# Edge scores of a graph layer: rings of six groups for four, and GpSimd's gathers written out

## The chip, the cores and the metric

The kernel runs on one core of one Trainium2 chip. Its engines are TensorE (PE), VectorE (DVE), ScalarE (ACT), GpSimd (POOL) and SyncE (SP, which here only issues DMAs). The metric is the device time of one execution in microseconds (us). The median of three runs is 2775.32 us (2767.02 to 2775.95).

## The reference, cut to what matters

The kernel computes two layers over a graph of 3125 nodes and 53125 edges, the edges sorted by their target node:

```python
x = x + _L0_gnn_ref(_layernorm(x), edge_index, edge_attr_64, ...)
x = x + _L0_ffn_ref(_layernorm(x)[None], ...)[0]
x = x + _L1_gnn_ref(_layernorm(x), ..., src, dst)
x = x + _L1_ffn_ref(_layernorm(x)[None], ...)[0]
```

Only the first of these, the attention over edges, has the stage that changes:

```python
Q = (x @ Wq).reshape(N, 8, 32); K = (x @ Wk).reshape(N, 8, 32)
score = (Q[src] * K[tgt]).sum(axis=-1) * scale + edge_attr @ We
```

A softmax over the edges of each target, a weighted sum of V rows and the other three parts follow. The change leaves them as they are.

## The kernel before, in words

The stage before has written the query rows to DRAM (`q_rows`, 3125 rows of 1 KB) and the key rows, split into three bf16 parts and packed by rank, to `k_rows`. It has put the source nodes of all edges into SBUF as `src_t`: 128 partitions by 86 groups by 5 indices. Then comes the edge stage, lines 658 to 944. 128 edges stand one per partition, and five such columns make one group of 640 edges; there are 84 groups (`NK`). Every engine but SP runs a loop of 21 turns of four groups (`EITER`, `GI`), and SP three pieces of such a loop. The buffers that carry a group are rings of four: `qr` (query rows), `ea` and `eaT` (edge attributes and their transposes), `loc` (places of key rows) and the one-hot tiles `oh_lo` and `oh_hi`.

One group n goes like this:

- ACT waits until DVE has freed group n-2 (wait at L812), copies the 5 indices of group n+2 from `src_t` to the ring `src_s` (L788, "staging") and signals GpSimd. Then it copies the transposed edge attributes out of PSUM (L816, L817), makes its half of the key one-hots of group n+1 (L797, L801), and copies the score of the edge attributes (L823).
- GpSimd waits for the staged indices and issues five indirect DMAs (L766), each of which gathers 128 query rows of 1 KB into `qr`. Since ACT stages in program order, a gather of group n+2 starts only after ACT has finished group n-1. The gathers of groups 0 and 1 (L368) belong to the stage before.
- PE loads five start positions into registers (L845), transposes the edge attributes (L852), selects key rows with 20 one-hot matmuls into three PSUM banks of `psK` (L864), multiplies the edge attributes by We (L873) and counts source nodes (L879).
- DVE makes its half of the key one-hots (L899) and the counting one-hots (L927, L929), waits for the gathered rows and for each bank of `psK`, multiplies `qr` by it in place (L934, three per group) and adds up each head (L939). That last instruction raises `s_free`, which frees the group's slot.
- SP loads the edge attributes of group n (L724, L725, L727) when PE has transposed group n-4, and `loc` of group n+1 (L735).

At the start of the stage SP and ACT also load the key rows into SBUF (`kp`, L711).

The order of the work is fixed by the order of the code on each engine and by semaphores; no planner chooses it.

Of the kernel before, what the change touches and what calls it, by code (L numbers as in the profile page):

```python
# [6 lines left out]
BF16 = mybir.dt.bfloat16  # L7
# [22 lines left out]
AHEAD = 2  # L30
R = 42
# [38 lines left out]
def build(nc, x, src, dst, edge_attr_64, L0_gnn_Wq, L0_gnn_Wk, L0_gnn_Wv, L0_gnn_We, L0_gnn_Wo, L0_gnn_bo,  # L70
# [7 lines left out]
    def sb_high(ctx, name, shape, dt=F32):  # L78
        return ctx.enter_context(nc.sbuf_tensor(name, shape, dt, side="right"))
# [4 lines left out]
    def sem(name):  # L84
        return top.enter_context(nc.semaphore(name))
# [7 lines left out]
    with top:  # L93
# [567 lines left out]
        s_webd, s_ea = sem1("we_loaded"), [sem1(f"ea{g}_loaded") for g in range(GI)]  # L661
        s_staged, s_open = sem1("indices_staged"), sem1("gathers_open")
        s_loc = [sem1(f"locals{g}_loaded") for g in range(GI)]
# [7 lines left out]
        with ExitStack() as st:  # L671
            we2 = sb(st, "we2", [2 * ED, 2 * H])
            src_s = sb(st, "src_s", [E, GI, G], I32)
            kp = sb(st, "kp", [3 * R, KB, D], BF16)
            loc = sb(st, "loc", [3 * R, GI, G * E], BF16)
# [5 lines left out]
            ea = sb(st, "ea", [E, GI, G * ED])  # L681
            eaT = sb(st, "eaT", [128, GI, 3 * E])
# [4 lines left out]
            oh_lo = sb(st, "oh_lo", [E, GI, G, P], BF16)  # L687
            oh_hi = sb(st, "oh_hi", [E, GI, G, T], BF16)
# [12 lines left out]
            K_SLOT = (0, 1, 0, 1)  # L701
# [13 lines left out]
            def _(sp):  # L715
# [4 lines left out]
                def load_ea(i, g, tail):  # L720

                    at = bass.ds((i * GI * G + g * G) * ED, G * ED)
                    sp.wait_ge(s_ead, i * GI + g + 1)
# [22 lines left out]
                with sp.Fori(last_i + 1, EITER) as i:  # L746
# [12 lines left out]
            @block.gpsimd  # L759
            def _(pool):  # L760
                def gather(n, g):

                    pool.wait_ge(s_staged, n + g - AHEAD + 1)
                    pool.sem_inc(s_open, 1)
                    for u in range(G):
                        nc.gpsimd.indirect_dma_start(  # L766
                            out=qr[:, g, u, :], out_offset=None, in_=q_rows,
                            in_offset=bass.IndirectOffsetOnAxis(ap=src_s[:, g, u:u + 1], axis=0)).then_inc(s_got[g], 16)

                for g in range(AHEAD, GI):  # L770
                    gather(0, g)
                with pool.Fori(1, EITER) as i:
                    for g in range(GI):
                        gather(i * GI, g)

                for s in sems0:
                    pool.sem_clear(s)

            @block.scalar
            def _(act):  # L780
# [3 lines left out]
                act.sem_inc(s_eae, GI)  # L784
                act.sem_inc(s_esk, GI)

                def stage(at, g):
                    nc.scalar.activation(src_s[:, g, :], src_t[:, at, :].rearrange("p a u -> p (a u)"), ACT.Copy)\  # L788
                      .then_inc(s_staged, 1)

                def k_onehots(slot, k_slot, turn):

                    act.wait_ge(s_loc[slot], 16 * (turn + 1))
                    act.wait_ge(s_kta, turn * GI + slot + GI)
# [4 lines left out]
                    act.wait_ge(s_kabs, turn * GI + slot + 1)  # L799
# [4 lines left out]
                act.sem_inc(s_kta, GI)  # L804
# [4 lines left out]
                with act.Fori(0, EITER) as i:  # L809
                    for g in range(GI):  # L810
# [12 lines left out]
                        nc.scalar.activation(score[:, :, bass.ds(i * GI * G + g * G, G)].rearrange("p h u -> p u h"),  # L823
# [12 lines left out]
            def _(pe):  # L836
# [4 lines left out]
                pe.sem_inc(s_ead, GI)  # L841
                pe.sem_inc(s_ohu, GI)
                with pe.Fori(0, EITER) as i:
                    for g in range(GI):
                        _, first = nc.values_load_multi_w_load_instructions(  # L845
                            base_i[0:1, bass.ds(i * GI * G + g * G, G)], engines=[mybir.EngineType.PE], min_val=0, max_val=KB - CB)

                        pe.wait_ge(s_ea[g], 48 * (i + 1))
                        pe.wait_ge(s_eae, i * GI + previous_use(g, 2, GI) + 1 + GI)
# [6 lines left out]
                        pe.wait_ge(s_kt, i * GI + g + 1 + GI)  # L856
                        pe.wait_ge(s_kta, i * GI + g + 1 + GI)
                        if g in K_GROUPS:
                            pe.wait_ge(s_kp[K_GROUPS.index(g)], 48)
                        for m, (a, b) in enumerate(BANKS):  # L860
                            pe.wait_ge(s_kfree, (i * GI + g) * 3 + m + 1)
# [7 lines left out]
                        pe.wait_ge(s_eae, i * GI + g + 1 + GI)  # L869
                        pe.wait_ge(s_esk, i * GI + previous_use(g, 2, GI) + 1 + GI)  # L870
# [6 lines left out]
                        pe.wait_ge(s_oh, i * GI + g + 1)  # L877
# [7 lines left out]
                pe.wait_ge(s_free, GI + NK)  # L885
# [8 lines left out]
            def _(v):  # L894
# [7 lines left out]
                v.sem_inc(s_free, GI)  # L902
# [15 lines left out]
                v.sem_inc(s_kt, GI)  # L918
                v.sem_inc(s_kfree, 3)
                k_onehots(0, K_SLOT[0], 0)  # L920
                with v.Fori(0, EITER) as i:
                    for g in range(GI):
# [9 lines left out]
                        for m, (a, b) in enumerate(BANKS):  # L932
                            v.wait_ge(s_kx, (i * GI + g) * 3 + m + 1)
# [3 lines left out]
                        v.wait_ge(s_kfree, (i * GI + g) * 3 + 6)  # L937
# [1217 lines left out]
```

## Time and profile before

| | |
|---|---|
| median of three runs | 2775.32 us |
| profiled execution, its span | 2767.3 us |
| fastest of the three runs | 2767.02 us |
| edge stage, from first gather L766 to last | 165.6 to 857.4 us |
| mean granted clock of TensorE over the span | 0.724 of full |

The profile shows one execution. Its own time is its span of 2767.3 us, which is within 0.3 us of the fastest run, so nothing of note lies around the span. A timeline row gives the start of an instruction, its length, its engine, its line and tiles, and in brackets how long the engine had been idle before it and what ended that. "remote" means that a semaphore ended the wait and the profile does not name a sender that had just finished. "issue" means that it waited for nothing that the profile shows. The time of a gather is the time in which GpSimd writes its descriptors; its data move later.

### The profile page before, as it was taken

How to read it: one execution, taken by the hardware profiler on the slowest of the kernel's cores; microseconds unless marked ns; L12 is line 12 of the kernel's file. 1: busy time of each engine (PE TensorE's matmuls, PEld its weight loads, DVE VectorE, ACT ScalarE, POOL GpSimd, SP SyncE). 2: the span in 40 equal slices, each digit the busy share in tenths (PEclk: the TensorE clock that was granted, in tenths of full speed). 3: DMA queues.
4: the chain of work that ended last, by engine and by line, in shares of the span. 5: the costliest groups of instructions: out<-in, count | busy, mean ns of one | idle time of the engine just before them, and what ended most of it. 6: DMA issues, size and time to landing. Idle time of an engine off the chain costs nothing. (4 is left out here: it accounts for less than half of the span.)

```text
span 2767.3 us, 37014 instructions
## 1 busy us (share of the span) xinstructions
PE 1553.5 (56%) x9103; PEld 1290.4 (47%) x9104; DVE 1112.4 (40%) x2670; ACT 770.1 (28%) x1831; POOL 1089.8 (39%) x1126
## 2 busy tenths in 40 slices
PE   6347777777786478699940000000004747999992
PEld 5235555555564356489940000000003647999992
DVE  6335555555554743211133333333334773112123
ACT  4234444444443134233411000000000123334440
POOL 0635555555662020022215666666665001222220
PEclk9757666666656689799975555555556958999996
DMA  4384443444443310066644455555553017999997
GB/s 122 97 156 114 116 117 114 113 120 111 119 118 89 82 35 28 6 194 193 207 130 153 165 187 193 180 167 176 168 197 109 0 47 257 335 341 347 336 344 196
DMA packets 264204, 434.41 MB, mean 157 GB/s; under 512 B 36520, under 2 KB 203960, under 8 KB 264039
## 3 DMA queue, kind: packets, MB, share of 16 engines
q1 hardware_dynamic: 203011, 289.15, 32.6%
q0 software_dynamic: 54768, 141.45, 17.5%
q10 hardware_dynamic: 6388, 3.39, 0.7%
q8 instruction: 15, 0.25, 0.0%
q14 instruction: 22, 0.18, 0.0%
HBM read 342.48 MB, written 91.37 MB: 157 GB/s over the span
## 5 line engine op out<-in xcount | busy, mean ns | idle before, releaser
L766 POOL DMA_INDIRECT qr<-q_rows,src_s x410 | 404.1, 986 | 328.8 <-ACT src_s L788 219.5
L1796 POOL DMA_INDIRECT fr<-f_rows,src_s x420 | 407.0, 969 | 259.1 <-ACT src_s L1787 129.7
L2079 PE MATMUL psO<-acc,carry_on 128*125 128x256 f32 x50 | 21.9, 620 | 692.9 <-DVEq L1975 677.4
L864 PE MATMUL psK<-kp,oh_k 126*128 x1680 | 351.9, 373 | 68.6 <-issue 67.8
L1816 DVE SCALAR_TENSOR_TENSOR acc<-acc,same,fr 128x256 f32<-128x256 f32 x420 | 203.6, 485 | 413.4 <-issue 262.1
L2079 PEld LDWEIGHTS psO<-acc,carry_on 128*125 128x125 f32 x50 | 15.4, 321 | 699.0 <-DVEq L1975 677.8
L864 PEld LDWEIGHTS psK<-kp,oh_k 126*128 126x128 bf16 x1680 | 217.1, 129 | 194.6 <-issue 114.8
L934 DVE TENSOR_TENSOR qr<-qr,psK 128x512 f32<-128x512 f32 (+1 forms) x252 | 141.0, 594 | 299.4 <-remote 190.5
L1617 PEld LDWEIGHTS m1psH<-m1xT,m1w 128*128 128x128 f32 x1792 | 211.4, 194 | 2.8
L1617 PE MATMUL m1psH<-m1xT,m1w 128*128 128x128 f32 x1792 | 211.6, 277 | 0.0
L1629 PE MATMUL m1psY<-m1w,m1hT 128*128 128x256 f32 x896 | 203.4, 380 | 1.0 <-issue 0.6
L1597 ACT ACTIVATE m1hT<-m1psH,m1par 128x128 f32<-128x128 f32 x448 | 128.1, 369 | 249.4 <-PE m1psH L1617 169.4
L1787 ACT ACTIVATE src_s<-src_i 128x5 int32 x84 | 17.5, 208 | 583.8 <-DVEq L1823 293.5
L1629 PEld LDWEIGHTS m1psY<-m1w,m1hT 128*128 128x128 f32 x896 | 165.8, 190 | 23.1 <-issue 2.2
L1571 POOL DMA_INDIRECT y<-m1yr,m1to x56 | 54.8, 979 | 289.6 <-DVE m1yr L1680 289.6
L797 ACT ACTIVATE dist<-loc,k_neg 126x640 bf16<-126x640 bf16 x170 | 130.9, 821 | 31.7 <-DMA loc<-locals_ 31.7
L852 PE MATMUL psE<-ident,ea 128*128 128x128 f32 (+1 forms) x252 | 63.2, 378 | 130.1 <-issue 110.5
L939 DVE TENSOR_REDUCE dots<-qr 128x1280 f32 x84 | 125.0, 1488 | 18.6 <-DVE qr L934 14.4
L1617 PEld LDWEIGHTS m0psH<-m0xT,m0w 128*128 128x128 f32 x1024 | 120.9, 194 | 1.5
L1617 PE MATMUL m0psH<-m0xT,m0w 128*128 128x128 f32 x1024 | 121.0, 277 | 0.0
L801 ACT ACTIVATE oh_k<-dist,ones 126x1280 bf16<-126x1280 bf16 x85 | 115.8, 1363 | 10.1
L1629 PE MATMUL m0psY<-m0w,m0hT 128*128 128x256 f32 x512 | 115.8, 379 | 0.0
(447 smaller groups left out, 2456.4 us busy)
## 6 DMA issues: line engine op xcount, KB each, us to landing
m1w<-in_L_ffn_W_dram SPq DMA_DIRECT2D x112, 1024.0 KB
run_rows<-acc SPq DMA_DIRECT2D x84, 640.0 KB
m0w<-in_L_ffn_Wd_dram SPq DMA_DIRECT2D x32, 1024.0 KB, 5.5
loc<-locals_ SPq DMA_DIRECT2D x85, 157.5 KB
ea<-in_edge_attr_dram SPq DMA_DIRECT2D x84, 140.0 KB
yt<-y SPq DMA_DIRECT2D x15, 560.0 KB
m1b<-in_L_ffn_b_dram SPq DMA_DIRECT2D x56, 128.0 KB
fr<-f_rows,src_s POOLq DMA_INDIRECT x420
```

Of the source, the lines that this page charges most:

```text
L766: nc.gpsimd.indirect_dma_start(out=qr[:, g, u, :], out_offset=None, in_=q_rows, in_offset=bass.IndirectOffsetOnAxis(ap=src_s[:, g, u:u + 1 ...
L797: last = nc.scalar.activation(dist[:, c - CD, :], loc[:, slot, :], ACT.Abs, bias=k_neg[:, c:c + 1])
L801: nc.scalar.activation(oh_k[:, k_slot, CD:CB, :], dist[:], ACT.Relu, bias=ones[0:3 * R, 0:1], scale=-1.0)\
L852: last = nc.tensor.transpose(psE[0:w, g % 2, n * E:(n + 1) * E], ea[:, g, n * 128:n * 128 + w], ident[:])
L864: last = nc.tensor.matmul(psK[:, m, (u - a) * D:(u - a + 1) * D], oh_k[:, K_SLOT[g], c, u * E:(u + 1) * E], kp[:, bass.ds(first[u] + c, 1) ...
L934: nc.vector.tensor_tensor(qr[:, g, a:b].rearrange("p u d -> p (u d)"), qr[:, g, a:b].rearrange("p u d -> p (u d)"), psK[:, m, 0:(b - a) * ...
L939: nc.vector.tensor_reduce(dots[:, :, at].rearrange("p h u -> p u h"), qr[:, g].rearrange("p u (h d) -> p u h d", h=H), AX.X, ALU.add).then ...
L1597: last = nc.scalar.activation(hT[s][:, m, :], psH[s][:, m * 128:(m + 1) * 128], ACT.Gelu, bias=par[s][:, m:m + 1] if own_w1 else b1_0[:, m ...
L1617: last = nc.tensor.matmul(psH[s][:, m * 128:(m + 1) * 128], w1[s if own_w1 else 0][:, k, m * 128:(m + 1) * 128], xT[s][:, k, :], start=(k ...
L1629: last = nc.tensor.matmul(psY[:, s, 0:D], hT[s][:, m, :], w2[s][:, m, :], start=(m == 0), stop=(m == KC - 1))
L1796: nc.gpsimd.indirect_dma_start(out=fr[:, g, u, :], out_offset=None, in_=f_rows, in_offset=bass.IndirectOffsetOnAxis(ap=src_s[:, g, u:u + 1 ...
L1816: ins = nc.vector.scalar_tensor_tensor(acc[:, g, u, :], acc[:, n // G % GI, n % G, :], same[:, bass.ds(i * GI * G + g * G + u, 1)], fr[:, ...
```

## The change

Six groups take the place of four in the rings and loops of the edge stage (`GB`, `BITER` for `GI`, `EITER`): 14 turns of six. `src_s` and ACT's staging go. GpSimd's loop goes too: its 82 groups of five gathers stand in the program one after another, take their indices from `src_t` directly, and wait for `s_free`, that is, for DVE having freed group n-6. The later gather stage (L1796) keeps its rings of four.

```diff
 AHEAD = 2
+GB = 6
+BITER = NK // GB
...
-        s_got = [sem(f"rows{g}_gathered") for g in range(GI)]
+        s_got = [sem(f"rows{g}_gathered") for g in range(GB)]
         qr_ctx = ExitStack()
-        qr = sb_high(qr_ctx, "qr", [E, GI, G, D])
+        qr = sb_high(qr_ctx, "qr", [E, GB, G, D])
...
-        s_staged, s_open = sem1("indices_staged"), sem1("gathers_open")
-        s_loc = [sem1(f"locals{g}_loaded") for g in range(GI)]
+        s_webd, s_ea = sem1("we_loaded"), [sem1(f"ea{g}_loaded") for g in range(GB)]
+        s_loc = [sem1(f"locals{g}_loaded") for g in range(GB)]
...
-            src_s = sb(st, "src_s", [E, GI, G], I32)
-            loc = sb(st, "loc", [3 * R, GI, G * E], BF16)
+            loc = sb(st, "loc", [3 * R, GB, G * E], BF16)
...
-            ea = sb(st, "ea", [E, GI, G * ED])
-            eaT = sb(st, "eaT", [128, GI, 3 * E])
+            ea = sb(st, "ea", [E, GB, G * ED])
+            eaT = sb(st, "eaT", [128, GB, 3 * E])
...
-            oh_lo = sb(st, "oh_lo", [E, GI, G, P], BF16)
-            oh_hi = sb(st, "oh_hi", [E, GI, G, T], BF16)
+            oh_lo = sb(st, "oh_lo", [E, GB, G, P], BF16)
+            oh_hi = sb(st, "oh_hi", [E, GB, G, T], BF16)
...
-            K_SLOT = (0, 1, 0, 1)
+            K_SLOT = (0, 1) * (GB // 2)
...
-                    sp.wait_ge(s_kt, i * GI + g + 2)
-                    sp.wait_ge(s_kta, i * GI + g + 2)
-                    sp.dma_start(loc[:, (g + 1) % GI, :], locals_[bass.ds((i * GI + g + 1) * G * E, G * E)]
-                                 .partition_broadcast(3 * R)).then_inc(s_loc[(g + 1) % GI], 16)
-
-                last_i, last_g = REST // G // GI, REST // G % GI
+                    sp.wait_ge(s_kt, i * GB + g + 2)
+                    sp.wait_ge(s_kta, i * GB + g + 2)
+                    sp.dma_start(loc[:, (g + 1) % GB, :], locals_[bass.ds((i * GB + g + 1) * G * E, G * E)]
+                                 .partition_broadcast(3 * R)).then_inc(s_loc[(g + 1) % GB], 16)
...
             def _(pool):
-                def gather(n, g):
-
-                    pool.wait_ge(s_staged, n + g - AHEAD + 1)
-                    pool.sem_inc(s_open, 1)
+                for n in range(AHEAD, NK):
+                    pool.wait_ge(s_free, n + 1)
                     for u in range(G):
-                        nc.gpsimd.indirect_dma_start(
-                            out=qr[:, g, u, :], out_offset=None, in_=q_rows,
-                            in_offset=bass.IndirectOffsetOnAxis(ap=src_s[:, g, u:u + 1], axis=0)).then_inc(s_got[g], 16)
-
-                for g in range(AHEAD, GI):
-                    gather(0, g)
-                with pool.Fori(1, EITER) as i:
-                    for g in range(GI):
-                        gather(i * GI, g)
+                        nc.gpsimd.indirect_dma_start(out=qr[:, n % GB, u, :], out_offset=None, in_=q_rows,
+                                                     in_offset=bass.IndirectOffsetOnAxis(ap=src_t[:, n, u:u + 1], axis=0))\
+                          .then_inc(s_got[n % GB], 16)
 
                 for s in sems0:
                     pool.sem_clear(s)
...
-                def stage(at, g):
-                    nc.scalar.activation(src_s[:, g, :], src_t[:, at, :].rearrange("p a u -> p (a u)"), ACT.Copy)\
-                      .then_inc(s_staged, 1)
...
-                with act.Fori(0, EITER) as i:
-                    for g in range(GI):
-
-                        act.wait_ge(s_free, i * GI + g + AHEAD + 1)
-                        act.sem_inc(carrier, 1)
-                        stage(bass.ds(i * GI + g + AHEAD, 1), (g + AHEAD) % GI)
-                        act.wait_ge(s_ead, i * GI + g + 1 + GI)
+                with act.Fori(0, BITER) as i:
+                    for g in range(GB):
+                        act.wait_ge(s_ead, i * GB + g + 1 + GB)
                         nc.scalar.activation(eaT[:, g, 0:2 * E], psE[:, g % 2, 0:2 * E], ACT.Copy)
                         nc.scalar.activation(eaT[0:ED, g, 2 * E:3 * E], psE[0:ED, g % 2, 2 * E:3 * E], ACT.Copy)\
                           .then_inc(s_eae, 1)
 
-                        k_onehots((g + 1) % GI, K_SLOT[(g + 1) % GI], i + (g + 1) // GI)
-                        act.wait_ge(s_es, i * GI + g + 1)
+                        k_onehots((g + 1) % GB, K_SLOT[(g + 1) % GB], i + (g + 1) // GB)
+                        act.wait_ge(s_es, i * GB + g + 1)
...
-                        pe.wait_ge(s_eae, i * GI + g + 1 + GI)
-                        pe.wait_ge(s_esk, i * GI + previous_use(g, 2, GI) + 1 + GI)
+                        pe.wait_ge(s_eae, i * GB + g + 1 + GB)
+                        pe.wait_ge(s_esk, i * GB + previous_use(g, 2, GB) + 1 + GB)
...
-                v.sem_inc(s_free, GI)
+                v.sem_inc(s_free, GB)
...
-                with v.Fori(0, EITER) as i:
-                    for g in range(GI):
-                        at = bass.ds(i * GI * G + g * G, G)
-
-                        k_onehots((g + 1) % GI, K_SLOT[(g + 1) % GI], i + (g + 1) // GI)
-                        v.wait_ge(s_ohu, i * GI + g + 1)
+                with v.Fori(0, BITER) as i:
+                    for g in range(GB):
+                        at = bass.ds(i * GB * G + g * G, G)
```

Wherever the diff is cut, `GI` becomes `GB` and `EITER` becomes `BITER` in the same way.

On GpSimd, the edge stage before is this. `indices_staged` is ACT's signal, and L777 clears semaphores:

```order
L759 UNCONDITIONAL_BRANCH [waits barrier_Pool_Activation_PE_DVE_SP_gather]
L766 DMA qr<-q_rows,src_s 128x256 [waits indices_staged]
L766 DMA qr<-q_rows,src_s 128x256 x4
...
L772 UNCONDITIONAL_BRANCH
L772 ISA
L766 DMA qr<-q_rows,src_s 128x256 [waits indices_staged]
L766 DMA qr<-q_rows,src_s 128x256 x4
...
L763 REGISTER_ALU
L766 DMA qr<-q_rows,src_s 128x256 [waits indices_staged]
L766 DMA qr<-q_rows,src_s 128x256 x4
...
L772 REGISTER_ALU
L772 COMPARE_AND_BRANCH
L777 ISA x50
```

After the change the stage is 82 times the same five gathers without a branch; the wait is DVE's `rows_free`:

```order
L759 UNCONDITIONAL_BRANCH [waits barrier_Pool_Activation_PE_DVE_SP_gather]
L764 DMA qr<-q_rows,src_t 128x256 [waits rows_free]
L764 DMA qr<-q_rows,src_t 128x256 x4
...
L764 DMA qr<-q_rows,src_t 128x256 [waits rows_free]
L764 DMA qr<-q_rows,src_t 128x256 x4
L769 ISA x50
L672 UNCONDITIONAL_BRANCH
```

So GpSimd no longer waits for ACT, and its instructions stand once for each group where before four groups stood in a loop.

On ACT, the first group of the loop before, from the start of the loop to the score:

```order
L809 UNCONDITIONAL_BRANCH
...
L788 ISA [waits rows_free]
L788 ACTIVATE src_s<-src_t 128x5
...
L816 ACTIVATE eaT<-psE 128x256 [waits ea_turned]
L817 ACTIVATE eaT<-psE 64x128
...
L797 ACTIVATE dist<-loc,k_neg 126x640 [waits locals1_loaded,k_onehots_act]
...
L801 ACTIVATE oh_k<-dist,ones 126x1280 [waits k_distances]
...
L823 ISA [waits edge_score_done]
L823 ACTIVATE score<-psS 128x5x8
```

and after:

```order
L797 UNCONDITIONAL_BRANCH
...
L800 ACTIVATE eaT<-psE 128x256 [waits ea_turned]
L801 ACTIVATE eaT<-psE 64x128
...
L785 ACTIVATE dist<-loc,k_neg 126x640 [waits locals1_loaded,k_onehots_act]
...
L789 ACTIVATE oh_k<-dist,ones 126x1280 [waits k_distances]
...
L807 ISA [waits edge_score_done]
L807 ACTIVATE score<-psS 128x5x8
```

The wait for `rows_free` and the staging copy are gone from ACT; everything behind them moves up.

## Rows read from the trace of the kernel before

**Rows 1.** The page: engines (busy, share, instructions), and the group of gathers

```profile
PE 1553.5 (56%) x9103; PEld 1290.4 (47%) x9104; DVE 1112.4 (40%) x2670; ACT 770.1 (28%) x1831; POOL 1089.8 (39%) x1126
...
L766 POOL DMA_INDIRECT qr<-q_rows,src_s x410 | 404.1, 986 | 328.8 <-ACT src_s L788 219.5
```

**Rows 2.** Waits, 160 to 875 us: who waited for whom, total us, times, longest

```profile
POOL qr L766 <- ACT src_s L788: 219.5, 56, 40.1
DVE qr L934 <- remote: 190.5, 39, 9.4
...
POOL qr L766 <- issue: 109.3, 354, 1.2
```

**Rows 3.** Tile qr: count, min/median/max ns, first and last start

```profile
L766 POOL DMA_INDIRECT qr<-q_rows,src_s x410: 943/949/1602, 165.6 to 857.4; - x137
...
L939 DVE TENSOR_REDUCE dots<-qr x84: 1487/1489/1491, 167.4 to 871.3; 128x1280 f32 x84
```

**Rows 4.** Timeline of POOL, 530 to 562 and 566 to 576 us

```profile
531.12 0.95 POOL L766 DMA_INDIRECT qr<-q_rows,src_s  x1 [2.10 <-ACT src_s L788]
...
542.40 0.95 POOL L766 DMA_INDIRECT qr<-q_rows,src_s  x1 [0.30 <-issue]
549.08 0.95 POOL L766 DMA_INDIRECT qr<-q_rows,src_s  x1 [5.72 <-ACT src_s L788]
...
557.67 0.94 POOL L766 DMA_INDIRECT qr<-q_rows,src_s  x1 [2.64 <-ACT src_s L788]
...
569.40 0.95 POOL L766 DMA_INDIRECT qr<-q_rows,src_s  x1 [0.30 <-issue]
```

**Rows 5.** Timeline of DVE, the same stretches

```profile
545.51 1.62 DVE L934 TENSOR_TENSOR qr<-qr,psK 128x512 f32<-128x512 f32 x3 [7.78 <-remote]
547.35 1.49 DVE L939 TENSOR_REDUCE dots<-qr 128x1280 f32 x1 [0.22 <-DVE qr L934]
...
556.88 1.49 DVE L939 TENSOR_REDUCE dots<-qr 128x1280 f32 x1 [0.22 <-DVE qr L934]
...
561.72 1.49 DVE L939 TENSOR_REDUCE dots<-qr 128x1280 f32 x1 [0.22 <-issue]
...
571.95 1.62 DVE L934 TENSOR_TENSOR qr<-qr,psK 128x512 f32<-128x512 f32 x3 [7.23 <-remote]
```

**Rows 6.** Timeline of ACT, 534 to 562 us

```profile
544.65 0.38 ACT L816 ACTIVATE eaT<-psE 128x256 f32<-128x256 f32 x1 [8.41 <-remote]
...
548.10 0.20 ACT L788 ACTIVATE src_s<-src_t 128x5 int32 x1
```

**Rows 7.** Timeline of PE, 525 to 562 us

```profile
528.91 0.87 PE L852 MATMUL psE<-ident,ea 128*128 128x128 f32 x3 [1.92 <-issue]
...
535.72 0.88 PE L852 MATMUL psE<-ident,ea 128*128 128x128 f32 x3
```

**Rows 8.** Start of the stage: timeline of all engines, 120 to 182 us

```profile
161.84 0.90 PE L852 MATMUL psE<-ident,ea 128*128 128x128 f32 x3 [15.71 <-DMA ea<-in_edge_attr_dram]
```

**Rows 9.** Window: PE, PEld, DVE, ACT, POOL busy, granted clock, DMA share, GB/s

```profile
146.00:162.00 16.00, 0.28 (x2) 0.19 (x3) 0.00 (x0) 0.00 (x0) 0.00 (x0) 0.50 1.08 168
```

**Rows 10.** DMA queues, 160 to 872 us: packets, MB, share of 16 engines

```profile
q0 software_dynamic: 19680, 53.77, 26.9%
...
q14 instruction: 2, 0.02, 0.0%
```

**Rows 11.** Gathers written out, next stage: timeline of all engines, 955 to 994 us

```profile
983.76 1.23 PE L185 MATMUL psT<-ident,tile_a 125*128 125x125 f32 x10
...
988.89 1.34 ACT L193 ACTIVATE tT<-psT 128x500 f32<-128x500 f32 x3 [11.01 <-remote]
```

**Rows 12.** First written-out gathers, L368: timeline of all engines, 66 to 100 us

```profile
69.75 1.12 POOL L368 DMA_INDIRECT qr<-q_rows,src_t  x1 [62.02 <-DMA q_rows<-x]
...
80.73 0.95 POOL L368 DMA_INDIRECT qr<-q_rows,src_t  x1 [0.30 <-issue]
80.82 0.19 DVE L588 TENSOR_TENSOR pre<-pre,has_in 125x25 f32<-125x25 f32 x1
```

More of the change, by code:

```diff
@@ L783, in _ @@
                 act.dma_start(we2[ED:2 * ED, H:2 * H], L0_gnn_We).then_inc(s_webd, 16)
-                act.sem_inc(s_eae, GI)
-                act.sem_inc(s_esk, GI)
-                def stage(at, g):
-                    nc.scalar.activation(src_s[:, g, :], src_t[:, at, :].rearrange("p a u -> p (a u)"), ACT.Copy)\
-                      .then_inc(s_staged, 1)
+                act.sem_inc(s_eae, GB)
+                act.sem_inc(s_esk, GB)
                 def k_onehots(slot, k_slot, turn):
                     act.wait_ge(s_loc[slot], 16 * (turn + 1))
-                    act.wait_ge(s_kta, turn * GI + slot + GI)
+                    act.wait_ge(s_kta, turn * GB + slot + GB)
                     act.sem_inc(carrier, 1)
@@ L798, in k_onehots @@
                     last.then_inc(s_kabs, 1)
-                    act.wait_ge(s_kabs, turn * GI + slot + 1)
+                    act.wait_ge(s_kabs, turn * GB + slot + 1)
                     act.sem_inc(carrier, 1)
@@ L808, in _ @@
                     load_k(act, n)
-                with act.Fori(0, EITER) as i:
-                    for g in range(GI):
-                        act.wait_ge(s_free, i * GI + g + AHEAD + 1)
-                        act.sem_inc(carrier, 1)
-                        stage(bass.ds(i * GI + g + AHEAD, 1), (g + AHEAD) % GI)
-                        act.wait_ge(s_ead, i * GI + g + 1 + GI)
+                with act.Fori(0, BITER) as i:
+                    for g in range(GB):
+                        act.wait_ge(s_ead, i * GB + g + 1 + GB)
                         nc.scalar.activation(eaT[:, g, 0:2 * E], psE[:, g % 2, 0:2 * E], ACT.Copy)
@@ L818, in _ @@
                           .then_inc(s_eae, 1)
-                        k_onehots((g + 1) % GI, K_SLOT[(g + 1) % GI], i + (g + 1) // GI)
-                        act.wait_ge(s_es, i * GI + g + 1)
+                        k_onehots((g + 1) % GB, K_SLOT[(g + 1) % GB], i + (g + 1) // GB)
+                        act.wait_ge(s_es, i * GB + g + 1)
                         act.sem_inc(carrier, 1)
-                        nc.scalar.activation(score[:, :, bass.ds(i * GI * G + g * G, G)].rearrange("p h u -> p u h"),
+                        nc.scalar.activation(score[:, :, bass.ds(i * GB * G + g * G, G)].rearrange("p h u -> p u h"),
                                              psS[:, g % 2, 0:G * H].rearrange("p (u h) -> p u h", h=H), ACT.Copy)\
@@ L840, in _ @@
                 nc.tensor.matmul(psC[0:P, 0:T], zb[:], zb[:, 0:T], start=True, stop=False, skip_group_check=True)
[L841 to L844, printed above, removed]
+                pe.sem_inc(s_ead, GB)
+                pe.sem_inc(s_ohu, GB)
+                with pe.Fori(0, BITER) as i:
+                    for g in range(GB):
                         _, first = nc.values_load_multi_w_load_instructions(
-                            base_i[0:1, bass.ds(i * GI * G + g * G, G)], engines=[mybir.EngineType.PE], min_val=0, max_val=KB - CB)
+                            base_i[0:1, bass.ds(i * GB * G + g * G, G)], engines=[mybir.EngineType.PE], min_val=0, max_val=KB - CB)
                         pe.wait_ge(s_ea[g], 48 * (i + 1))
-                        pe.wait_ge(s_eae, i * GI + previous_use(g, 2, GI) + 1 + GI)
+                        pe.wait_ge(s_eae, i * GB + previous_use(g, 2, GB) + 1 + GB)
                         for n in range(3):
@@ L917, in _ @@
                 dve_order.link(v, nc.vector.tensor_scalar(k_neg[:], k_at[:], -1.0, None, ALU.mult))
-                v.sem_inc(s_kt, GI)
+                v.sem_inc(s_kt, GB)
                 v.sem_inc(s_kfree, 3)
                 k_onehots(0, K_SLOT[0], 0)
-                with v.Fori(0, EITER) as i:
-                    for g in range(GI):
-                        at = bass.ds(i * GI * G + g * G, G)
-                        k_onehots((g + 1) % GI, K_SLOT[(g + 1) % GI], i + (g + 1) // GI)
-                        v.wait_ge(s_ohu, i * GI + g + 1)
+                with v.Fori(0, BITER) as i:
+                    for g in range(GB):
+                        at = bass.ds(i * GB * G + g * G, G)
+                        k_onehots((g + 1) % GB, K_SLOT[(g + 1) % GB], i + (g + 1) // GB)
+                        v.wait_ge(s_ohu, i * GB + g + 1)
                         nc.vector.tensor_tensor(oh_lo[:, g], iota_row[:].unsqueeze(1).to_broadcast([E, G, P]),
```

26 lines of the change are left out of this document (13 added, 13 removed).

## Prediction

> **What bounds the kernel now.** I read the page's shares first: no engine is busy for more than 56% of the span, so waits set the time, and the average over the stages says little of this one [rows 1]. Then I took the stage by itself. Its last result is the reduce of DVE, which frees a slot: 84 of them, the first starting at 167.4 us and the last at 871.3 [rows 3], 703.9 / 83 = 8.48 us per group. The list of waits of that stretch is next. DVE's longest waits stand before the multiply and end "remote"; no row there names a gather. So gathered rows are in time, and it is PE's products that are late. GpSimd waits for ACT's staging 56 times, 219.5 us, of which the longest, 40.1, lies ahead of its first gather [rows 2].
>
> That makes GpSimd a chain which adds up: 410 gathers x 0.986 us = 404.1 busy [rows 1], 109.3 of short gaps between them (354, 0.31 each) and 219.5 - 40.1 = 179.4 of waits [rows 2], together 692.8 us; the first gather starts at 165.6 and the last ends at 857.4 + 0.95 = 858.4 [rows 3], which is 692.8 too. 82 groups in 56 bursts are 1.46 groups per burst, with a mean pause of 3.2 us. Yet nobody waits for its rows. Why does the pace follow it? The timelines answer. A burst of two groups runs from 531.12 to 542.40 + 0.95 = 543.35 [rows 4]. In it PE's transposes begin at 535.72 and take 0.88 [rows 7], but ACT copies them only at 544.65, after 8.41 us of waiting that ends "remote" [rows 6], and DVE's multiply starts at 545.51 after 7.78 [rows 5]. The same after the next double burst: it ends at 569.40 + 0.95 = 570.35 [rows 4], the multiply starts at 571.95 [rows 5]. So what PE signals in a long burst arrives 2.16 and 1.60 us after its end. Signals of the first 4 us or so of a burst pass: transposes start 6.81 us apart (528.91, 535.72) across one burst's start [rows 7]. Between bursts and in a single one two reduces start 4.84 us apart (556.88, 561.72) [rows 5]. I read this as: descriptor writing on GpSimd holds up PE and its signals, and pauses are when the stage moves.
>
> **The change part by part.** The sum is against the profiled execution. Its span is 2767.3 us, its time equals the fastest of the three runs, 8 below the median 2775.32.
>
> *The staging on ACT goes*: 84 copies x 0.20 = 17 us of ACT [rows 6]. ACT is 28% busy [rows 1] and waits for PE's signal right behind each, so I cost it at nothing; were that cover gone, it would give back at most those 17 us.
>
> *Loops and rings of six.* 14 turns for 21 save 7 ends of turns per engine. No row shows one by itself; a group with such an end is within the 0.3 to 2 us of any "issue" gap [rows 4, 7], so 0 to 14 us, and PE's signals, not its issue, are waited for: I take 0. Loads of edge attributes may run six groups ahead instead of four; no wait of DVE names them. 0.
>
> *The first gathers move.* Today gather 2 starts at 165.6, after ACT has the loads behind it. Now slots 2 to 5 are free from the start, so 4 x 5 = 20 gathers go out as soon as GpSimd enters the stage, beside the loads of key rows. From 146 to 162 the DMA engines are full, 1.08 [rows 9], and PE's first transposes wait 15.71 us for edge attributes until 161.84 [rows 8]. A gather costs all 16 engines 26.9% x 712 us / 410 = 0.467 us [rows 10, 1], 20 of them 9.3. If they all go ahead of that load the stage starts 9.3 later, if behind it 0. I take the middle, 4.7, and keep both ends. The first reduce then ends at 167.4 + 1.49 + 4.7 = 173.6. The Trainium skill, "DMA: Bandwidth & Descriptors", section "Issuing engines are not separate DMA queues", says that DMAs started by the scalar, sync or gpsimd engine run on the same 16 engines and interleave. By that rule the shift would be nearer 9.3, and the result 4.6 later; no row here shows the two kinds side by side.
>
> *GpSimd's gate.* This is the term that decides. Today the pause ends when ACT stages, that is, when ACT has got through group n-1. In the new order it ends when DVE has freed group n-6. Per gather nothing changes: 0.986 and a 0.31 gap. Behind the waiting gather only gathers are queued, so the wait harms nobody by itself. But GpSimd, which today gets one group or two per staging, will write whatever slots are free. It reaches the full ring early (20 gathers at the start) and from there each reduce lets one group go. A group is 5 x 1.295 = 6.5 us of writing. The first reduce after a pause starts a burst 0.8 us later (today the staging copy ends at 548.30 and the gather starts at 549.08 [rows 6, 4]). The second reduce comes 4.8 to 6.8 us behind it, at DVE's free pace or PE's: before the first group is written out. So the burst doubles. The third group's products are signalled later than 4 us into the burst, and by the rows above they arrive after its end. So I expect bursts of two groups, always: 82 - 4 = 78 groups in 39 bursts. A pause is then 1.9 (mean of 2.16 and 1.60) for the signal, 3.3 from the multiply to the end of the reduce (545.51 to 547.35 + 1.49 = 548.84 [rows 5]), and 0.8 to the first gather: 6.0 us, against a mean of 3.2 today, where staging precedes the reduce.
>
> The sum: 78 x 5 x 0.986 = 384.5 busy; 351 gaps x 0.309 = 108.4; 38 pauses x 6.0 = 228.0; together 720.9. From the first gated gather, 173.6 + 0.8 = 174.4, to 895.3. Then 1.9 + 3.3 to the reduce that this burst held up, 900.5, and five groups still ahead with no gathers beside them, at PE's 6.8: 934.5. Today the stage's last reduce ends at 872.8. That is 61.7 later: 2767.3 + 61.7 = 2829.0. What follows waits for that reduce, so I let it pass on in full.
>
> Bounds of this term. If every burst is a single group whose successor is late, two in three groups cost 6.5 + 3.0, 9.5 each: about 20 more, 2849. If the pause is what it is today, 3.2, the 38 pauses lose 106 and the gain of the lookahead shows: 2723.
>
> **Rivals.**
> *B, bursts of three groups.* Six slots may let DVE free two slots in the pause. 26 bursts have 25 pauses: 13 fewer x 6.0 = 78, 2751. For it: the third reduce comes at 4.8 after the second if its products were finished before the burst [rows 5]. Against: the double burst of 531 held its second group's products back for 7.78 us.
> *C, the stall goes.* Perhaps it comes from GpSimd's loop or from the semaphores of the staging, and not from writing descriptors. Then PE's 6.8 per group bounds: 78 x 6.8 + 34 = 564 from 173.6, 738, 135 earlier: 2632. For it: in the first written-out gathers, from 69.75 on, DVE still does small steps in order with one at 80.82 while gathers go out [rows 12]. Against: these steps wait for DVE itself, and in the written-out gathers of the next stage PE's transposes, 983.76 + 1.23, are copied by ACT only at 988.89, 3.9 us late, after 11.01 of waiting [rows 11].
> *D, the pace stays.* The lookahead isn't used, since no rows were waited for; PE's chain goes on at 8.48 and the later start (4.7) and faster end cancel: about 2767.
> *E, code loading, on the slower side.* PE's turn grows from four groups to six, from some 300 instructions to some 450. In this stage only two instruction packets were fetched on q14 [rows 10], so today's loop is resident. If six groups are not, each of 13 returns fetches two blocks. The rows have no duration for that; between a gather's gap of 0.31 and PE's issue gap of 1.92 [rows 2, 7] I take the middle, 1.1: 13 x 2 x 1.1 = 29: 2796 without other effects. It decides once a turn no longer stays resident. The Trainium skill, "Runtime: NRT & Kernel Launch", section "Instruction fetch mechanics", says that a taken branch whose target isn't in the current two-page window forces a fetch of the target page. By that rule a larger turn is the risk; the present trace shows a turn of 300 without such fetches.
>
> **How the numbers follow.** The double bursts have 0.50, B 0.18, C 0.14, D 0.13, E 0.05. The predicted time is that of the likeliest, 2829; its own range is 2800 (a pause of 5.3) to 2850. The range 2740 to 2865 holds it, E, D and B, and some 16 more for a start 4.6 later and single bursts; C and the lower bound of the pause are left out. About 0.3%, 8 us, is what a measurement of this kernel tells from no change. Faster: B and C, 0.32. Within: D, 0.13. Slower: the first and E, 0.55.
>
> **What would show it.** In the new trace GpSimd's waits name DVE's reduce, about 38 times with a mean near 6 us; its bursts are of ten gathers; the last gather ends near 895 and the last reduce near 934; DVE's waits before the multiply still end "remote", and PE's signals arrive 1.6 to 2.2 us after a burst. The first transposes come after 161.84 by up to 9.3. The forecast is wrong if bursts are longer than 20 us with DVE working on within them (B, C), if the pause is 3 us or less, or if PE's "issue" gaps grow at each sixth group with new instruction packets (E).

## The result and the profile after

The changed kernel takes 2805.8 us (median of four runs, 2804.6 to 2812.8), the kernel before, measured with it, 2771.2: 1.0144 times as long, 95% interval 1.0108 to 1.0179. It is slower by about 35 us. The profiled execution has a span of 2811.0 us against 2767.3.

First the waits of the stage, which ran from 137 to 910 us; the rows are those of 140 to 915 us (engine, line, what it waited for: total us, times, longest). They answer to [rows 2]:

```profile
POOL qr L764 <- DVE dots L923: 235.2, 50, 17.5
DVE qr L918 <- remote: 205.9, 46, 8.3
...
POOL qr L764 <- issue: 109.2, 358, 0.3
```

GpSimd now waits for DVE's reduce, 50 times, and DVE's wait for late signals has grown from 190.5 us in 39 waits to 205.9 in 46. The tile `qr` shows where the stage begins and ends (min, median, max ns; first and last start). These rows answer to [rows 3], and the page's row of the gathers to [rows 1]:

```profile
L764 POOL DMA_INDIRECT qr<-q_rows,src_t x410: 943/949/1374, 137.5 to 870.7; - x137
L923 DVE TENSOR_REDUCE dots<-qr x84: 1487/1489/1491, 178.1 to 908.2; 128x1280 f32 x84
```

```profile
L764 POOL DMA_INDIRECT qr<-q_rows,src_t x410 | 389.5, 950 | 352.5 <-DVE dots L923 235.2
```

The first reduce is 10.7 us later (178.1 for 167.4), the last one 36.9 later (908.2 for 871.3). In between the pace is 730.1 / 83 = 8.80 us per group for 8.48. The remaining 43.7 - 36.9 = 6.8 us of the profile's difference fall behind the stage, where the code is the same; from the last reduce's end to the span's end the two kernels and the six others profiled on chips of this kind take 1884 to 1901 us, so those 6.8 lie within the scatter of eight profiles.

Now the timeline of the changed kernel from 292 to 322 us, three groups in the pattern that returns through most of the stage (start, length, engine, work, idle time before and what ended it). It answers to [rows 4 to 7]. POOL and DVE:

```profile
292.90 1.49 DVE L923 TENSOR_REDUCE dots<-qr 128x1280 f32 x1 [0.22 <-DVE qr L918]
294.66 0.95 POOL L764 DMA_INDIRECT qr<-q_rows,src_t  x1 [5.55 <-DVE dots L923]
...
299.67 0.95 POOL L764 DMA_INDIRECT qr<-q_rows,src_t  x1 [0.30 <-issue]
301.80 0.42 DVE L918 TENSOR_TENSOR qr<-qr,psK 128x256 f32<-128x256 f32 x1 [1.47 <-remote]
302.45 1.49 DVE L923 TENSOR_REDUCE dots<-qr 128x1280 f32 x1 [0.22 <-DVE qr L918]
304.21 0.95 POOL L764 DMA_INDIRECT qr<-q_rows,src_t  x1 [3.59 <-DVE dots L923]
307.23 1.49 DVE L923 TENSOR_REDUCE dots<-qr 128x1280 f32 x1 [0.23 <-DVE qr L918]
...
315.50 0.94 POOL L764 DMA_INDIRECT qr<-q_rows,src_t  x1 [0.30 <-issue]
318.39 1.62 DVE L918 TENSOR_TENSOR qr<-qr,psK 128x512 f32<-128x512 f32 x3 [8.11 <-PE psK L848]
320.22 1.49 DVE L923 TENSOR_REDUCE dots<-qr 128x1280 f32 x1 [0.22 <-DVE qr L918]
321.98 0.95 POOL L764 DMA_INDIRECT qr<-q_rows,src_t  x1 [5.54 <-DVE dots L923]
```

and PE in the double burst:

```profile
308.30 1.86 PE L848 MATMUL psK<-kp,oh_k 126*128 x11
...
310.62 0.27 PE L848 MATMUL psK<-kp,oh_k 126*128 x1 [0.46 <-issue]
311.37 0.28 PE L848 MATMUL psK<-kp,oh_k 126*128 x1 [0.48 <-issue]
312.74 0.41 PE L848 MATMUL psK<-kp,oh_k 126*128 x2 [1.09 <-issue]
```

Read it downwards. The reduce that ends at 294.39 lets a burst of one group go, 294.66 to 300.62. The third multiply of the next group gets its signal 1.2 us after that burst, so the next reduce comes 9.55 us after the first, when GpSimd has been idle for 3.59. It opens a burst of two groups, since the reduce after that comes 4.78 us later, in time. In this burst PE gets through 11 of 20 key matmuls in 1.86 us, then needs 7.4 us for the other nine (310.62 to 318.04); DVE's multiply begins 318.39 - 316.44 = 1.95 us after the last gather has ended, though PE had started the products of the first bank ten us before. Here PE itself is late, and the signal with it; the run with the late first gathers, below, shows a signal that is late after PE was done. Then the reduce, and 0.27 us later the next burst. Three groups take 9.55 + 4.78 + 12.99 = 27.3 us; before, such a turn of three was 26.4 us, from the reduce at 547.35 to the one at 573.79.

### The profile page after: what moved, and what is told of

Same layout as the page of the kernel before. It is cut to its first block and busy times, and to the rows that moved or that the text cites. A ratio compares the mean times of both kernels' runs of the same rounds, so it can differ in the third digit from the quotient of the medians.

```text
span 2811.0 us, 36475 instructions
## 1 busy us (share of the span) xinstructions
PE 1571.4 (56%) x9103; PEld 1292.4 (46%) x9104; DVE 1116.1 (40%) x2670; ACT 756.1 (27%) x1747; POOL 1079.1 (38%) x1126
## 5 line engine op out<-in xcount | busy, mean ns | idle before, releaser
L764 POOL DMA_INDIRECT qr<-q_rows,src_t x410 | 389.5, 950 | 352.5 <-DVE dots L923 235.2
L848 PEld LDWEIGHTS psK<-kp,oh_k 126*128 126x128 bf16 x1680 | 209.8, 125 | 235.4 <-issue 157.7
L918 DVE TENSOR_TENSOR qr<-qr,psK 128x512 f32<-128x512 f32 (+1 forms) x252 | 142.3, 594 | 322.8 <-remote 205.9
L1601 PEld LDWEIGHTS m1psH<-m1xT,m1w 128*128 128x128 f32 x1792 | 211.3, 194 | 2.8
L1601 PE MATMUL m1psH<-m1xT,m1w 128*128 128x128 f32 x1792 | 211.5, 277 | 0.0
L1601 PEld LDWEIGHTS m0psH<-m0xT,m0w 128*128 128x128 f32 x1024 | 121.8, 196 | 1.6
L1601 PE MATMUL m0psH<-m0xT,m0w 128*128 128x128 f32 x1024 | 121.9, 279 | 0.0
```

The source lines that it names most:

```text
L764: nc.gpsimd.indirect_dma_start(out=qr[:, n % GB, u, :], out_offset=None, in_=q_rows, in_offset=bass.IndirectOffsetOnAxis(ap=src_t[:, n, u: ...
L848: last = nc.tensor.matmul(psK[:, m, (u - a) * D:(u - a + 1) * D], oh_k[:, K_SLOT[g], c, u * E:(u + 1) * E], kp[:, bass.ds(first[u] + c, 1) ...
L918: nc.vector.tensor_tensor(qr[:, g, a:b].rearrange("p u d -> p (u d)"), qr[:, g, a:b].rearrange("p u d -> p (u d)"), psK[:, m, 0:(b - a) * ...
L1601: last = nc.tensor.matmul(psH[s][:, m * 128:(m + 1) * 128], w1[s if own_w1 else 0][:, k, m * 128:(m + 1) * 128], xT[s][:, k, :], start=(k ...
```

## The experiments

Twelve runs were made; eight stand in the table, the others in the text. They fall into five groups, each on another chip and each beside the kernel before. It took 2769.1 and 2770.9 us on two of these chips and 2517.7, 2520.0 and 2523.3 on the other three. I call the first a "chip of 2770" and the others a "chip of 2520". None of the five was met twice, so whether the chip or a state that it was in makes the difference is not shown.

| kernel | before there | median us | ratio, 95% interval | us per group |
|---|---|---|---|---|
| rings of six, staging kept | 2769.1 | 2771.1 | 1.0005 (0.9987 to 1.0023) | 8.46 |
| rings of four, written out, reduce gate | 2769.1 | 2802.8 | 1.0132 (1.0105 to 1.0160) | 8.89 |
| changed kernel + score gate | 2769.1 | 2752.8 | 0.9941 (0.9916 to 0.9966) | 8.22 |
| changed kernel, first gathers late | 2769.1 | 2825.8 | 1.0212 (1.0187 to 1.0237) | 9.13 |
| rows of 256 bytes | 2770.9 | 2816.2 | 1.0160 (1.0135 to 1.0184) | 8.85 |
| score gate again | 2770.9 | 2752.9 | 0.9925 (0.9902 to 0.9949) | 8.23 |
| no gathers past the ring | 2517.7 | 2520.3 | 0.9999 (0.9972 to 1.0026) | 6.34 |
| changed kernel again | 2520.0 | 2530.6 | 1.0042 (1.0017 to 1.0068) | 6.37 |

**Rings of six alone.** ACT's staging and GpSimd's loop of the kernel before, in the rings and turns of the changed one:

```diff
-                for n in range(AHEAD, NK):
-                    pool.wait_ge(s_free, n + 1)
+                def gather(n, g):
+                    pool.wait_ge(s_staged, n + g - AHEAD + 1)
...
+                with pool.Fori(1, BITER) as i:
+                    for g in range(GB):
+                        gather(i * GB, g)
```

> Rings of six and 14 turns, but ACT's staging and GpSimd's loop as before. If the place of GpSimd's gate makes the change slow (my theory): bursts, pauses and pace as before, 8.4 to 8.5 us per group, within 8 us of the kernel before. If rings of six or the longer turns cost (rival): about 8.8 us per group and 25 to 35 us over before.

Measured: no difference from before, 8.46 us per group, 57 bursts with a mean pause of 3.23 us (before 56 and 3.29). GpSimd's wait for the staging is the same as in [rows 2]:

```profile
POOL qr L768 <- ACT src_s L790: 218.9, 56, 40.8
```

The depth of the rings and the longer turns cost nothing and bring nothing. The rival falls, and with it code loading in turns of six: in the window of [rows 10], 160 to 872 us, four instruction packets came on q14 here and seven in the changed kernel, for two before, where two blocks at each of 13 returns would be 26.

**Written out with rings of four.**

```diff
-                    pool.wait_ge(s_staged, n + g - AHEAD + 1)
+                for n in range(AHEAD, NK):
+                    pool.wait_ge(s_free, n + 1)
...
+                        nc.gpsimd.indirect_dma_start(out=qr[:, n % GI, u, :], ...
```

> Rings of four as before, GpSimd's gathers written out, indices in place, gate on DVE's reduce of group n-4. Theory (the gate is after the reduce, the depth does not matter): 8.8 us per group, the start later by about 5 us (10 early gathers for 20), 25 to 35 us over before. If depth six is what makes it slow: 8.4 to 8.5 us per group and no more than 5 over before.

Measured: 33.7 us over before, as forecast. 80 gated groups went in 53 bursts with a mean pause of 4.38 us; in the changed kernel 78 groups in 50 bursts, 4.44. So this half of the change makes the whole loss, with rings of four as with rings of six. It still has three parts: the code written out, the indices in place, and the gate. The next one parts them.

**The gate moved back.** One line on top of the changed kernel:

```diff
                     pool.wait_ge(s_free, n + 1)
+                    pool.wait_ge(s_esk, GB + n - AHEAD)
```

> The changed kernel with one more wait on GpSimd: group n also waits for ACT's score of group n-3, which is where ACT's staging stood. Theory: mean pause back from 4.4 to about 3.3 us, gathers still 0.95 us each, so 8.2 to 8.4 us per group and 5 to 25 us under before. Rival (written-out code or reading the indices in place is what costs): 8.8 us per group, as the changed kernel.

Measured: 16.3 us under before, and 18.0 under on another chip. Code written out and indices read in place stay, so neither is what costs: it is the gate. The start differs from the changed kernel's too, because only five gathers now go out early for 20, and the first reduce comes at 172.7 us for 178.1. That is 5 us; the pace, 8.22 us per group for 8.80, is 48. The waits of its stage, and three rows of its timeline where a burst begins:

```profile
POOL qr L765 <- ACT score L808: 180.6, 56, 26.4
DVE qr L919 <- remote: 157.8, 37, 9.3
```

```profile
424.83 0.24 ACT L808 ACTIVATE score<-psS 128x40 f32 x1 [1.19 <-PE psS L858]
425.75 1.49 DVE L924 TENSOR_REDUCE dots<-qr 128x1280 f32 x1 [0.22 <-DVE qr L919]
425.82 0.94 POOL L765 DMA_INDIRECT qr<-q_rows,src_t  x1 [2.44 <-ACT score L808]
```

The gather begins at 425.82, beside the reduce that starts at 425.75. With the reduce as the gate it would have begun after 427.24; with the 0.27 us seen above that is some 1.7 us later, an estimate. The mean pause is 2.90 us over 57 pauses of the gated part, less than before's 3.29. That no staging copy stands between ACT's signal and the gather any more fits this, but no run shows it by itself. This is the version that beats both kernels, on the chips of 2770; on those of 2520 it was not run.

**The first gathers later.**

```diff
+                pool.wait_ge(s_ead, GB + 1)
                 for n in range(AHEAD, NK):
```

> The changed kernel, but GpSimd's first gather of the stage waits for PE's first transposes. If the 20 early gathers delay the load of edge attributes: transposes back at 162 us for 172.5, and 5 to 11 us under the changed kernel (less than 10.7 where the 25 us burst then falls beside the first groups). If the later start has another reason: transposes still at 170 or later.

Measured: 1.0212 times before for the changed kernel's 1.0144, so some 19 us slower than it, outside both expectations in sign. The transposes did move, to 167.5 us, and the first reduce to 173.5 for 178.1. But now the first burst runs beside the work:

```profile
173.54 1.49 DVE L924 TENSOR_REDUCE dots<-qr 128x1280 f32 x1 [0.22 <-issue]
...
185.00 0.37 PE L849 MATMUL psK<-kp,oh_k 126*128 x1 [0.95 <-issue]
...
191.98 0.38 ACT L801 ACTIVATE eaT<-psE 128x256 f32<-128x256 f32 x1 [12.92 <-remote]
...
203.94 1.62 DVE L919 TENSOR_TENSOR qr<-qr,psK 128x512 f32<-128x512 f32 x3 [27.37 <-remote]
205.78 1.49 DVE L924 TENSOR_REDUCE dots<-qr 128x1280 f32 x1 [0.22 <-DVE qr L919]
```

```profile
168.64 1.04 POOL L765 DMA_INDIRECT qr<-q_rows,src_t  x1 [36.36 <-PE psE L837]
...
198.74 0.94 POOL L765 DMA_INDIRECT qr<-q_rows,src_t  x1 [0.30 <-issue]
```

25 gathers without a pause, 168.64 to 199.68, and one group takes 32.24 us; DVE's multiply waits 27.37 us and starts 4.3 us after the last gather. The rows that it multiplies had been gathered before the stage, and PE had done the last of its 20 products by 185.37, so here it is the signal that is late, by 18.6 us. The expectation had counted that cover only as a smaller gain. Not every signal waits for the end of the burst: ACT's copy of the transposes, which waited 12.92 us, still came inside it, at 191.98. In the changed kernel the same 20 gathers lie beside the loads, where PE had nothing to do.

SP is held up too. Its loads of edge attributes stand one behind the other with no wait between them:

```profile
192.12 0.32 SPq L724 DMA_DIRECT2D ea<-in_edge_attr_dram  x1
196.13 0.70 SPq L725 DMA_DIRECT2D ea<-in_edge_attr_dram  x1
...
204.47 0.32 SPq L724 DMA_DIRECT2D ea<-in_edge_attr_dram  x1
204.98 0.32 SPq L725 DMA_DIRECT2D ea<-in_edge_attr_dram  x1
```

4.01 us lie between the two in the burst and 0.51 behind it. These pairs measure the hold-up without PE. In the changed kernel their median is 0.51 us in the pauses and in the first 4 us of a burst (37 and 19 pairs), and 1.95, at most 3.34, later in a burst (21 pairs).

**What in the gathers holds PE up: writing or data?** Two kernels were to tell, one without gathers past the ring (so its scores are others), one with rows of a quarter (scores others too):

```diff
-                for n in range(AHEAD, NK):
+                for n in range(AHEAD, GB):
...
-                        v.wait_ge(s_got[g], G * 16 * (i + 1))
+                        v.wait_ge(s_got[g], G * 16)
```

> The changed kernel without the gathers of groups 6 to 83 (the slots keep their old rows, so the scores are others). Theory (GpSimd's writing of descriptors holds up PE and its signals): DVE's waits 'remote' before the multiply vanish, groups go at PE's 6.8 us or less, so the stage ends 130 to 200 us earlier than in the changed kernel. Rival (PE's own chain with one-hots bounds): 8 us or more per group.

```diff
+                        w = D if n < GB else D // 4
+                        nc.gpsimd.indirect_dma_start(out=qr[:, n % GB, u, 0:w], out_offset=None,
+                            in_=q_rows if n < GB else q_rows.rearrange("n (a d) -> (n a) d", a=4), ...
```

> The changed kernel, but from group 6 on each gather moves rows of 256 bytes for 1 KB (as many descriptors, a quarter of the data; the scores are others). If the writing of descriptors is what holds up the signals: 8.7 to 8.9 us per group, as the changed kernel. If the moving data are (DMA traffic beside the signals): well under that, 7 to 8 us per group, 60 to 150 us less in all.

Both ran on a chip on which the kernel before takes 2517.7 us, and both took the same as it (2520.3 and 2519.6, ratios 0.9999 and 0.9985, both intervals across 1). Such runs can't tell the two theories apart, because there nothing is held up. The narrow one ran again, with the changed kernel itself:

> The narrow rows (256 bytes for 1 KB from group 6 on, as many descriptors; the scores are others) once more, since f_narrow ran on a chip on which the kernel before itself took 2518 us and nothing was held up. If this chip takes 2770 us for the kernel before: 8.7 to 8.9 us per group if writing descriptors holds up signals, 7 to 8 if the moving data do. If it takes 2518: 6.3 to 6.5 us per group as there.

> The changed kernel itself, unchanged. On a chip on which the kernel before takes about 2770 us: 1.010 to 1.018 times before, 8.8 us per group. On one on which it takes about 2518 and no signal is late: PE's chain bounds, 6.3 to 6.5 us per group in both, the early gathers delay the start by some 5 us, so 0 to 8 us over before.

Again a chip of 2520: 2523.7 for the narrow one (1.0007, 0.9991 to 1.0023), and 2530.6 for the changed kernel, 1.0042 (1.0017 to 1.0068) times before. But its trace shows what the other kind of chip hides. Tile `qr`, and its timeline around 400 us, both of the changed kernel:

```profile
L923 DVE TENSOR_REDUCE dots<-qr x84: 1487/1487/1490, 172.7 to 701.4; 128x1280 f32 x84
```

```profile
404.56 1.49 DVE L923 TENSOR_REDUCE dots<-qr 128x1280 f32 x1 [0.22 <-DVE qr L918]
406.07 4.13 PE L848 MATMUL psK<-kp,oh_k 126*128 x20
406.44 1.02 POOL L764 DMA_INDIRECT qr<-q_rows,src_t  x1 [0.30 <-issue]
407.77 0.69 DVE L918 TENSOR_TENSOR qr<-qr,psK 128x512 f32<-128x512 f32 x1 [0.21 <-PE psK L848]
410.27 0.95 POOL L764 DMA_INDIRECT qr<-q_rows,src_t  x1 [0.30 <-issue]
410.88 1.49 DVE L923 TENSOR_REDUCE dots<-qr 128x1280 f32 x1 [0.22 <-DVE qr L918]
```

The same program, with gathers at the same 0.95 and 0.30 us and one burst of 360 of them: all 20 matmuls of a group run in 4.13 us beside it, DVE multiplies 0.21 us after its wait begins, none of DVE's waits before the multiply ends "remote", and a group takes 6.37 us. SP's pair of loads, 0.51 us apart, is never over 0.53 in that burst. The kernel without gathers needs 6.34: on this kind of chip they cost next to nothing.

The traces also say where the rest of the time between the two kinds lies. The changed kernel's profiled span is 2811.0 us on the one and 2521.8 on the other, 289.2 apart. 206.8 have come by the end of the edge stage (909.7 for 702.9). Most of the rest is the later gather stage, which the change leaves alone (first on the chip of 2770, then on the chip of 2520):

```profile
L1780 POOL DMA_INDIRECT fr<-f_rows,src_s x420: 945/949/1199, 1522.0 to 2130.2; - x140
```

```profile
L1780 POOL DMA_INDIRECT fr<-f_rows,src_s x420: 942/949/1209, 1306.0 to 1836.2; - x140
```

It takes 608 us for 530. The second layer's large matmuls (L1601), on the other hand, stretch over 403 us and 406. So nearly all of the difference lies in the two stages that are full of indirect gathers.

The next chip was one of 2770:

> The narrow rows (256 bytes for 1 KB from group 6 on, as many descriptors; the scores are others) a third time, for a chip on which signals are late. If the kernel before takes about 2770 us here: 8.7 to 8.9 us per group if writing descriptors holds up signals, 7 to 8 if the moving data do. If it takes 2518: 6.3 to 6.5 us per group as in the two runs before, which tells nothing new.

> The score gate (GpSimd's group n waits for ACT's score of group n-3) again. Where the kernel before takes about 2770 us: 0.992 to 0.997 times before, as c_score_gate. Where it takes about 2518: nothing waits for GpSimd or for late signals, only the start counts (5 early gathers for 20), so 0 to 5 us over before and at or just under the changed kernel's 1.004.

Narrow rows: 2816.2 us, 1.016 times before, 8.85 us per group, 54 bursts of the gated part with a mean pause of 4.32. The queue of the gathers moved a quarter of the bytes in as good as the same stretch, 180 to 900 us (first the changed kernel, then the narrow one; packets, MB, share of 16 engines):

```profile
q0 software_dynamic: 18720, 51.14, 25.2%
```

```profile
q0 software_dynamic: 12480, 12.80, 9.4%
```

and DVE's waits are what they were:

```profile
POOL qr L765 <- DVE dots L924: 244.3, 51, 17.5
DVE qr L919 <- remote: 181.4, 43, 8.3
```

390 gathers are 48 packets each with full rows and 32 with narrow ones, so packets fell by a third, bytes by three quarters and the engines' share from 25.2% to 9.4%, and the pace stayed. So the amount of data moved is not the cause. What stayed is the number of gathers and the time in which GpSimd writes them. That writing as such does it is the likeliest reading; the two stages above fit it, but it is not shown, since the kernel without gathers never met this kind of chip.

**A gate before each gather.**

```diff
                     for u in range(G):
+                        if n >= GB and u == 1:
+                            pool.wait_ge(s_oh, n - GB + 2)
+                        elif n >= GB and u > 1:
+                            pool.wait_ge(s_kfree, (n - GB + 1) * 3 + 3 + u - 1)
```

> The changed kernel with a gate before each gather from group 6 on: the first after DVE's reduce of group n-6, the second after its counting one-hots of group n-5, the other three after its three multiplies of group n-5. GpSimd then never writes more than DVE's progress has let go, so no burst of ten. If the delay depends on how long a burst runs on (past about 4 us): 6.8 to 8.0 us per group, 40 to 150 us under before. If it hits any signal beside writing: no better than the changed kernel, and slower where gathers start later, 8.8 to 9.5.

> The gate before each gather (reduce of group n-6, counting one-hots of n-5, the three multiplies of n-5) again. Where the kernel before takes about 2770 us: DVE, held up by a late signal, lets no further gather go, so bursts end sooner. If a signal waits only for the burst under way, 7 to 8 us per group and 40 to 120 us under before; if any writing near it delays it, 8.8 or more. Where the kernel before takes 2518: 6.46 us per group and 1.002 times before, as g_spread.

Both times it was a chip of 2520, with 2529.1 us (1.0024, 1.0001 to 1.0047) and 2527.0 us (1.0013, 0.9992 to 1.0033), 6.46 and 6.35 us per group. Where nothing is held up, spreading brings nothing. Whether it shortens the hold-up on the other kind stays open. My figure of 4 us, from which on signals are late, has SP's pairs above for it and no run that tests it.

## Why the prediction was right, and where its sizes were off

The direction and the mechanism held: no wait names the gathered rows, before or after, the end of the stage follows GpSimd's bursts, and to let a burst start only after the reduce makes the pauses longer. The score gate shows it from the other side: moving the gate turns 35 us of loss into 16 of gain, about 5 of it by the earlier start. The time lies inside the range; but it moved by 35 us, 44 in the profile, where the sum had 62. Term by term, in the profiled execution:

| term | forecast | measured | difference |
|---|---|---|---|
| first gated gather starts | 174.4 | 179.9 | +5.5 |
| 390 gathers, busy | 384.5 | 370.4 | -14.1 |
| gaps between them | 108.4 | 103.6 | -4.8 |
| pauses | 38 x 6.0 = 228.0 | 49 x 4.44 = 217.7 | -10.3 |
| from the last gather to the last reduce's end | 39.2 | 38.0 | -1.2 |
| last reduce ends | 934.5 | 909.7 | -24.8 |

*The pauses* were right in sum by two errors against each other. "So I expect bursts of two groups, always" failed: 28 of the 50 bursts are double, 22 single. I had put the second reduce 4.8 to 6.8 us behind the first; after a single burst's onset its third multiply waits for the burst's end, and it comes at 9.5 (292.90, 302.45 above). That case was my upper bound, where I made it cost 9.5 for two groups in three. The sum there is wrong: "about 20 more" needs 9.5 for every group (78 x 9.5 = 741 for 720.9), while two in three with the third at 4.8 give 619, less than the sum. In truth the 9.5 alternates with a free 4.78 and a held 12.99. And 6.0 for a pause was too much: after a double burst it is 5.51, since DVE's reduce releases the gather in 0.27 us where I had carried over the 0.8 from ACT's staging, and after a single one 3.13.

*The gathers* are 0.950 us each for 0.986. "Per gather nothing changes" was wrong by 14 us. Before, 31 of 410 take over 1.1 us, 1.38 on average, and all of them lie beside DVE's counting one-hots (L927); after, 2 do. Neither the loop nor the staged index explains it: with the score gate, code written out and indices in place, 23 are long again. The place in DVE's round where a burst begins may be what decides; that is not shown, for 79 gathers of the changed kernel lie beside those one-hots and only the 2 are long.

*The start.* I took 4.7 us between 0 and 9.3. The first reduce came 10.7 later. From the first load of key rows (132.8 before, 137.3 after) to PE's first transposes it is 35.3 us for 29.0, so the 20 early gathers cost 6.3. Rings of six with the old gate take 28.7, the narrow rows with their 20 early gathers 35.0, which agrees. The other 4.4 stand ahead of the stage and are not theirs: the first four kernels of the table, on one chip, begin that load at 138.9 to 140.5, whatever they do later. The load of edge attributes was pushed aside:

```profile
172.54 0.90 PE L836 MATMUL psE<-ident,ea 128*128 128x128 f32 x3 [20.83 <-DMA ea<-in_edge_attr_dram]
```

20.83 us for 15.71 [rows 8]. With five early gathers, under the score gate, the stretch is 27.1. Gathers started by GpSimd delay a load started by SP: that agrees with what the Trainium skill says ("DMA: Bandwidth & Descriptors", "Issuing engines are not separate DMA queues"), that DMAs started by different engines share the same 16. The 6.3 us lie between the 4.7 that I took and the 9.3 of that rule.

*The rivals.* Bursts of three never came. The pace that stays (D) is what the ring alone gives, not the gate. Code loading (E) is refuted by the rings of six with the old gate, at 1.0005. C, that the hold-up is gone and PE bounds, did not happen where the result was measured, but it is what chips of 2520 do, at 6.37 us per group for my 6.8. I had the hold-up as a property of the kernel; it is one of the kernel on some chips.

## What to carry to other kernels

A producer that nobody waits for can still set the pace, by what its work does to the others' signals: then ask when its bursts begin and what else runs beside them, not whether its results are in time. A deeper ring and leave to run ahead brought nothing here, because nobody was waiting for the product; where the hold-up is the loss, release each burst from the earliest event that is safe, and put the long one beside loads. Time a tuning step on several chips, each against the kernel before: the change's loss is 1.4% on one kind and 0.4% on the other.

## What the runs showed of the hardware

- The same kernel takes 2770 us on some chips and 2520 on others; its runs on one chip spread by 1.1% or less. For the changed kernel the edge stage has 8.80 us per group for 6.37, and that stage and the later gather stage make up 280 of the 289 us between its two profiles.
- On the slower kind, PE's matmuls, signals and SP's DMA issues are held up beside a burst of indirect gathers: 20 matmuls in 9.7 us (308.30 to 318.04) for 4.13, two loads of SP 1.95 us apart for 0.51, and a multiply 1.95 us after the end of a burst of 10, 4.3 after one of 25, with rows of 1 KB. With rows of 256 bytes the pace is the same, 8.85 us per group.
- The granted clock of TensorE over the edge stage was 0.66 in the changed kernel on the slower kind (200 to 850 us) and 0.78 on the other (200 to 650 us). It does not make the difference in the later gather stage, where PE did nothing and had 0.50 on both.
- GpSimd itself is alike on both: 0.95 us for a gather and 0.30 between two.
